# A grouped convolution in front of a routed linear layer: the first tiles convolved in plain float32, and the first three steps in another order

## What is computed

```python
out = lax.conv_general_dilated(x, weight, window_strides=(1,), padding=[(4, 4)],
                               dimension_numbers=('NCH', 'OIH', 'NCH'), feature_group_count=4)
y = out + einsum('nd,od->no', c, c_weight)[:, :, None] + bias[None, :, None]
base_out = einsum('btd,od->bto', y, base_W) + base_b            # 512 -> 512
probs = softmax(einsum('btd,nd->btn', y, router_W) + router_b)  # 15 routes
topk_p, topk_i = top_k(probs, 8)
w = einsum('btk,btke->bte', topk_p, onehot(expert_map[topk_i]))
h = einsum('btd,erd->bter', y, A)                               # 8 experts, rank 16
result = x + base_out + einsum('bter,eor->bto', h * w[..., None], B) * 2.0
```

## Time and profile before

| | us |
|---|---|
| median of 3 runs | 187.44 |
| lowest and highest | 187.42, 187.69 |
| the profiled execution | 188.49 |
| its span, first to last instruction | 186.7 |
| TensorE busy in it | 180.1 |
| DVE, POOL, ACT busy | 156.2, 143.9, 82.9 |

### The profile page before, as it was taken

One profiled execution on the slowest core, in us unless ns is written; L12 is line 12 of the kernel. 1 busy time (PEld: TensorE's weight loads), 2 busy tenths in 40 slices (PEclk: granted clock), 3 DMA queues, 4 the chain that ended last, 5 costly groups with the idle time before them and its releaser, 6 DMA issues.

```text
span 186.7 us, 3948 instructions
## 1 busy us (share of the span) xinstructions
PE 180.1 (96%) x1243; PEld 171.8 (92%) x1243; DVE 156.2 (84%) x513; ACT 82.9 (44%) x249; POOL 143.9 (77%) x141
## 2 busy tenths in 40 slices
PE   7889999999999999999999999999999999999992
PEld 2469979999999999999999999999999999999992
DVE  0997999989888888888888888889888889978673
ACT  3687344454343545444344545434354544422310
POOL 2639979988898888888988888879888887895410
PEclk9999999999999999999999999999999999999998
DMA  6999642755745454645555464754645631233313
GB/s 185 387 312 328 191 158 80 227 169 180 219 137 165 137 186 167 228 169 190 151 153 176 135 217 169 225 170 123 207 125 177 243 98 68 97 112 112 116 56 112
DMA packets 17733, 32.01 MB, mean 171 GB/s; under 512 B 1969, under 2 KB 2865, under 8 KB 17713
## 3 DMA queue, kind: packets, MB, share of 16 engines
...
## 4 chain that ended last, share of the span: by engine, by line
PE 88%; DVE 4%; DMA 2%; issue 2%; ACT 2%; DVEq 0%; SPq 0%
PE wide_ps L619 58%; PE wide_ps L655 11%; PE conv_banks L605 10%; PE edge_bank L605 2%; DMA wide_sb<-wide_w 2%; PE odd_bank L642 2%; PE conv_banks L619 2%; PE conv_banks L566 2%; ACT wide_hi L350 1%; DVE xr L768 1%; DVE y_lo L887 1%; DVE y L859 0%; PE conv_banks L655 0%; DVE y_rows L774 0%; ACT y_hi L394 0%
## 5 line engine op out<-in xcount | busy, mean ns | idle before, releaser
L619 PE MATMUL wide_ps<-wide_hi,y_hi 128*128 128x400 f32 (+1 forms) x248 | 79.2, 325 | 1.3 <-ACT y_hi L394 0.7
L619 PE MATMUL wide_ps<-wide_hi,y_lo 128*128 128x400 f32 (+1 forms) x248 | 75.9, 312 | 0.0
L619 PE MATMUL wide_ps<-wide_lo,y_hi 128*128 128x400 f32 (+1 forms) x248 | 75.9, 312 | 0.0
L496 POOL TENSOR_TENSOR terms_lo<-terms,terms_hi 128x512 fp32r<-128x512 f32 x28 | 36.3, 1298 | 18.6 <-ACT terms_hi L379 18.5
L619 PEld LDWEIGHTS wide_ps<-wide_hi,y_hi 128*128 128x128 f32 x248 | 46.3, 188 | 3.9 <-ACT y_hi L394 1.1
L619 PEld LDWEIGHTS wide_ps<-wide_lo,y_hi 128*128 128x128 f32 x248 | 46.5, 189 | 0.0
L619 PEld LDWEIGHTS wide_ps<-wide_hi,y_lo 128*128 128x128 f32 x248 | 46.4, 188 | 0.0
L491 POOL TENSOR_TENSOR xr<-xr,base_b_sb 128x512 f32<-128x512 f32 x32 | 41.9, 1310 | 3.8 <-DMA xr<-x_rows 3.8
L514 POOL TENSOR_TENSOR y_lo<-y,y_hi 128x512 fp32r<-128x512 f32 x29 | 37.5, 1295 | 3.2 <-ACT y_hi L394 3.2
L401 ACT ACTIVATE hw_hi<-odd_bank 128x128 fp32r<-128x128 f32 x31 | 8.6, 277 | 52.7 <-PE odd_bank L642 52.7
L768 DVE TENSOR_TENSOR xr<-wide_ps,xr 128x512 f32<-128x512 f32 x30 | 20.7, 691 | 5.4 <-PE wide_ps L655 4.1
...
## 6 DMA issues: line engine op xcount, KB each, us to landing
...
conv_sb<-conv_w ACTq DMA_DIRECT2D x2, 128.0 KB, 4.5
```

The costliest lines, as they stand in the source:

```text
L496: nc.gpsimd.tensor_tensor(terms_lo[i % 2][:, :, :, :], terms[i][:, :, :, :], terms_hi[i % 2][:, :, :, :].bitcast(F32), ALU.subtract)\
L619: mm = nc.tensor.matmul(sums_of(t, k)[:, b, 0:columns[1] - columns[0]], a[k % 2][:, r, :], w[:, r, columns[0]:columns[1]], start=r == 0 an ...
```

## The change

Tiles 0 to 3 are convolved from `x_in` and `conv_sb` as they were loaded, in plain float32: two matmuls a tile instead of six. `x_hi`, `x_lo` and the split of the weight blocks that only these tiles use are gone (`conv_hi` and `conv_lo` have 10 blocks instead of 14, with their own numbering `S_*`). The condition inputs and the weight blocks are one tensor in memory, so ACT issues one DMA of 450 columns where there were two of 256 and 194, and then piece 1. The condition weights are spread by ACT, group 0 apart; group 0's condition matmul stands between the two of tile 0, and `condition_first(0)` waits for that group alone. The first `y_hi` is a copy on DVE. `wide_lo` of run 0 is made on POOL. `up_lo`, one DVE instruction before, is a subtraction on POOL from `up_scaled`, a second scaled copy that ACT makes. `y_lo` of tile 2 is made on POOL. SP issues weight piece 3 before `x_in` 3, and `terms` 4 after a wait for the last `wide` run. The warm-up has eight matmuls. The other pieces are a new order of the first three steps; `isinstance(t, int)` was always true.

```diff
-WARM_UP = 9
+WARM_UP = 8
...
-W_OWN, W_REACH = (0, 2, 4, 6), (1, 3, 5, 7)
+W_OWN, W_REACH = (1, 2, 5, 6), (0, 3, 4, 7)
...
+COND = N + C + GROUPS + 2 * ROUTES
+W_PIECES = (slice(0, COND + 2 * P), slice(COND + 2 * P, COND + 4 * P),
+            slice(COND + 4 * P, COND + 8 * P), slice(COND + 8 * P, COND + 11 * P),
+            slice(COND + 11 * P, COND + 14 * P))
...
+S_OWN, S_SUM, S_QUARTERS, S_ALL = (0, 1, 5, 6), (2, 3, 7, 8), (4, 9), 10
+S_PIECES = ((slice(0, 2), slice(1, 3), (0, 1)), (slice(2, 5), slice(8, 11), (3,)),
+            (slice(5, 7), slice(5, 7), (2,)), (slice(7, 10), slice(11, 14), (4,)))
...
             load_x(2)
             sync.wait_ge(wide_in[1], 16)
+            load_conv(3)
             load_x(3)
+            sync.wait_ge(wide_in[3], 16)
             load_terms(START, 0)
-            sync.wait_ge(wide_in[3], 16)
-            load_conv(3)
             load_edges(START // 2, 0)
...
+            def cond_weights(groups):
+                nc.scalar.copy(cond_w_sb[:, groups, :, :],
+                               cond_w_in_sb[:, groups, :].unsqueeze(2)
+                               .to_broadcast([P, groups.stop - groups.start, BP, CG]))\
+                    .then_inc(cond_w_ready, 1)
...
+            act.wait_ge(conv_w_in[0], 16)
+            cond_weights(slice(0, 1))
+            cond_weights(slice(1, GROUPS))
+            wide_high(range(1))
+            bias_condition(range(1), 1)
...
             odd_up(START, 0)
-            y_high(1, 1)
-            conv_high(3)
-            bias_condition(1)
+            y_high(1, 1, 2)
+            bias_condition(range(2, GROUPS), 3)
             exponentials(0, 0)
             terms_high(START, 0)
             act.wait_ge(up_in, 16)
             nc.scalar.activation(up_hi[:, :], up_sb[:, :], ACT.Copy, scale=LORA_SCALE)\
                 .then_inc(up_hi_ready, 1)
+            nc.scalar.activation(up_scaled[:, :], up_sb[:, :], ACT.Copy, scale=LORA_SCALE)\
+                .then_inc(up_scaled_ready, 1)
             edge_high(START // 2, 0)
...
-                    conv_high(4)
+                if t == 1:
+                    conv_high(2)
...
+            pool.wait_ge(wide_hi_ready, 1)
+            wide_low_part(nc.gpsimd, 0, wide_lo_first)
...
+            def up_low():
+                pool.wait_ge(up_scaled_ready, 1)
+                pool.wait_ge(up_hi_ready, 1)
+                nc.gpsimd.tensor_tensor(up_lo[:, :], up_scaled[:, :], up_hi[:, :].bitcast(F32),
+                                        ALU.subtract).then_inc(up_lo_ready, 1)
+
+            conv_low(0)
+            conv_low(1)
             edge(START // 2, 0)
-            conv_low_later(3)
 
             def step(t, k, p, q):
-                if isinstance(t, int) and t == 0:
+                if t == 0:
                     terms_low(t + 4, k)
+                    up_low()
                     edge_low(p + 2, k // 2)
                     pool.wait_ge(base_b_in, 16)
                     bias_rows(t, k)
+
+                    y_low(t + 2, k + 2, 3)
                     return
-                if isinstance(t, int) and t == 1:
+                if t == 1:
+                    terms_low(t + 4, k)
                     bias_rows(t, k)
-                    terms_low(t + 4, k)
                     edge(p + 3, 1 - k // 2)
-
-                    y_low(t + 2, k + 2, 4)
-                    conv_low_later(4)
+                    y_low(t + 2, k + 2)
+                    conv_low(2)
+                    conv_low(3)
...
+            def conv_first(t):
+
+
+
+                own, reach = t % 2, 1 - t % 2
+                nc.tensor.matmul(first_ps[:, t % 2, :, :], conv_sb[:, W_OWN[t], :],
+                                 x_in[t][:, :, own:own + BLK], start=True, stop=False)
+                if t == 0:
+                    cond_sums(range(1), 1)
+                nc.tensor.matmul(first_ps[:, t % 2, :, :], conv_sb[:, W_REACH[t], :],
+                                 x_in[t][:, :, reach:reach + BLK], start=False, stop=True)\
+                    .then_inc(conv_done, 1)
...
-                    pe.wait_ge(odd_ready, 1)
+                    pe.wait_ge(odd_ready, 2)
...
+            for t in range(2):
+                pe.wait_ge(conv_w_in[t], 16)
+                pe.wait_ge(x_loaded[t], 16)
+                conv_first(t)
+            cond_sums(range(1, 2), 2)
+
+            def conv_later(t):
+                pe.wait_ge(y_rows_ready, t - 1)
+                pe.wait_ge(conv_w_in[2], 16)
+                pe.wait_ge(x_loaded[t], 16)
+                conv_first(t)
 
             def first_step():
                 runs = range(RUNS)
-                pe.wait_ge(y_hi_ready, 1)
+                pe.wait_ge(y_hi_first, 1)
                 for r in runs:
                     pe.wait_ge(wide_hi_ready, r + 1)
                     linear(0, 0, (r,), products=(HIGH,))
...
+                cond_sums(range(2, GROUPS), 2)
+                conv_later(2)
...
+                    pe.wait_ge(out_added, t - 1)
+                    if t == 2:
+                        pe.wait_ge(y_hi_ready, t + 1)
+                        linear(t, k, runs, (FRONT_BANK,), (HIGH,))
+                        linear(t, k, runs, (FRONT_BANK,), (W_REST,))
+                        pe.wait_ge(y_lo_ready, t + 1)
+                        linear(t, k, runs, (FRONT_BANK,), (Y_REST,)).then_inc(front_done, 1)
...
+            dve.wait_ge(conv_w_in[0], 16)
...
+            dve.wait_ge(cond_biased, 1)
             condition_first(0)
             turn(0, 0)
+            dve.wait_ge(y_ready, 1)
+            nc.vector.tensor_copy(y_hi[0][:, :, :], y[0][:, :, :]).then_inc(y_hi_first, 1)
+            y_low(0, 0)
             wide_low(1)
-            y_low(0, 0)
             wide_low(2)
             wide_low(3)
+            dve.wait_ge(cond_biased, 2)
             condition_first(1)
             turn(1, 1)
-            y_low(1, 1)
             choose(0, 0)
             dve.wait_ge(logits_ready, 1)
             best(0, 0)
...
-                    dve.wait_ge(up_hi_ready, 1)
-                    nc.vector.scalar_tensor_tensor(out=up_lo[:, :], in0=up_sb[:, :],
-                                                   scalar=LORA_SCALE,
-                                                   in1=up_hi[:, :].bitcast(F32), op0=ALU.mult,
-                                                   op1=ALU.subtract).then_inc(up_lo_ready, 1)
-                    hw_low(0, 0)
-                    y_low(2, 2)
                     dve.wait_ge(top_ready, 2)
                     mark(1, 1)
+                    condition_first(3)
+                    hw_low(0, 0)
+                    return
+                if t == 1:
                     difference(START + 1, 1)
-                    return
-                if isinstance(t, int) and t == 1:
+                    turn(3, 3)
                     add_out(0, 0)
                     weigh(1, 1)
-                    condition_first(3)
-                    turn(3, 3)
```

253 lines of the change are left out of this document (86 added, 167 removed).

## The result

| | before | after |
|---|---|---|
| median, runs on one chip | 187.7 | 186.8 |
| lowest and highest | 187.22, 188.39 | 185.62, 188.09 |
| ratio after / before | | 0.994 [0.9925, 0.9955] |
| profiled execution | 188.49 | 186.31 |
| its span | 186.7 | 184.5 |

The change makes the kernel faster, by 0.45 to 0.75%. The profiled execution, though, was forecast at 186.4 and took 186.31. So the document has two questions: which steps held inside the trace, and why the timed runs gained less than the pair of traces.

A forecast was written before the change was run, and what follows sets the result against it. TensorE's own work (96% busy) was taken to bound the steady part, so the start's gain would last: step 4, set by POOL, at 33.7 instead of 35.81, 2.1 us off the median 187.44, gives 185.3, range 184.6 to 186.8.

The forecast's parts named there:

- First weights and first linear: Start of the kernel: merged 450-column weight piece lands at 4.8 us, first `linear` matmul starts at 9.1 instead of 10.56.
- The cast on DVE: First `y_hi`, 0.43 us on DVE against 0.63 on ACT, plus 0.2 us held up by POOL's instruction.
- Plain convolutions: Tiles 0 to 3 on TensorE: 0.88 us per 512-column float32 matmul, 1.76 per tile against 1.43, +0.33 us each.
- Step 0 and 1: Reordered start on TensorE: `linear(0)` done at 12.75, tile 3 at 18.9; `turn_hw(0)`'s wait for `odd_up(5)` covered by 0.2 us.
- Step 2: On TensorE: begins at 22.2 instead of 24.05, without the wait for `add_out`, and lasts 5.13 us.
- Step 3: On TensorE: lasts 5.48 us, the length of a later odd step, against 5.74 before.
- Step 4: POOL's `y_lo(4)` sets its start at 33.7, after TensorE's 33.0, against 35.81 before; chance 0.42.
- The sum: Whole kernel: 35.81 - 33.7 = 2.1 us less, taken off the median 187.44, gives 185.3; profiled execution 186.4.
- The collision at `conv_lo(1)`: POOL's 384 columns start between DVE's `wide_lo(2)` and `wide_lo(3)`, delaying the latter 1.0 us: 186.3 us; chance 0.20.
- the rival of the clock: TensorE stays at the lower pace through tiles 0 and 1, +3.5 us there: 188.8 us; chance 0.06.
- The late landing: Merged weight piece lands at 5.5 or after, 0.7 us on the chain, POOL's stretch 18.6: 186.8 us; chance 0.09.
- POOL is not late: POOL's stretch under 17 us or started a microsecond sooner, so TensorE's own path decides: 184.6 us; chance 0.17.

The follow-up runs named there:

- the other four traces: The changed kernel profiled again, unaltered; these profiled executions took 187.03, 187.0, 186.64 and 187.76 us.
- POOL relieved: Changed kernel with POOL's `y_lo(4)` put ahead of `bias_rows(3)` in the fourth step (t == 3) alone: 186.75 us, ratio 0.9934 to the kernel before.
- TensorE relieved by 0.46 at step 3: Changed kernel with the old place of `odd_up(5)` back, `turn_hw(0)` waiting for `odd_up(4)` only: 186.57 us, ratio 0.9924 to the kernel before.
- the repeated trace: The kernel before, run again unaltered for a second trace: 188.05 us; profiled execution 187.82, span 186.0.

## Why the prediction was right inside one trace and wrong in the number

**First weights and first linear.** Forecast 4.8 and 9.1, measured 4.55 and 8.92. The merged piece landed 3.8 us after its issue, like the small one of the earlier trace rows (3.6). The cast on DVE was not held up (0.43 us; POOL's instruction ended at 8.50). That `y` was ready at 8.44, forecast 8.4, was luck: the weights came 0.25 early, and tile 0's first matmul took 0.2 too long. In the other four traces the first `linear` began at 9.18 to 10.06.

**Plain convolutions.** A record is 0.43 us (512-column rows 0.86 a matmul), forecast 0.44; the 128-column row was the right base.

**Step 0 and 1.** `linear(0)` ended at 12.77 (forecast 12.75). `turn_hw(0)`, covered by 0.2 in the forecast, waited 0.22, and in other executions nothing or 0.16 to 0.79: `odd_up(5)` stands behind `y_high(2)` on ACT, forecast at 18.7 and done at 19.18, as `odd_up(4)` before them had waited for its load. The cover was a matter of landing, and was too thin to be counted.

**Step 2.** Forecast 22.2, measured 22.59: the wait above, and step 1's own length. It took 5.14, as said.

**Step 3** was costed at 5.48 and took 5.81. This is a mis-sized term: it was taken from a later odd step, and here `up` waits for `hw_lo`, which stands behind the turn on DVE. Before had the same stall, in its 5.74.

**Step 4** was to be set by POOL at 33.7. POOL's stretch began at 15.95 (forecast 15.9) and took 17.28 (17.8), so y_lo(4) ended at 33.23, and TensorE's own chain ended at 33.54. The number came out by luck, as TensorE was 0.5 later than forecast and POOL 0.5 sooner; the mechanism was a tie that TensorE led. With POOL relieved nothing moved. With TensorE relieved by 0.46 at step 3, 0.27 was left at step 4, which began 0.15 behind POOL's y_lo(4).

**The sum.** The profiled execution was forecast at 186.4 and took 186.31; the four other traces of the changed kernel read 186.64 to 187.76, so that hit too is in part luck. The step that failed is "35.81 - 33.7 = 2.1 us less" with "the gain is taken off the median: 185.3". Both starts of step 4 were taken as one moment. The traces showed 35.81 and 35.22 in the kernel before, and 33.54 to 34.87, 34.1 on average, in the changed one: a gain of 1.4 us. The 2.1 was the gain against a late execution of before (188.49, typical 188.01), with a wait for `add_out` that the repeated trace does not have; on the side of after it held nothing for the slow first matmul and the collision. And it was subtracted from the median of three early executions (187.44). From 185.34 to the typical 186.66 it is 1.32 us: 0.57 for the median of three (188.01 - 187.44), 0.48 for the late trace of before, 0.35 for the trace of after, which was an early one (186.66 - 186.31), less 0.08 by which the pair of traces gained more than 2.1. The 1.05 us between the profiled execution and the median, which the table of before shows, was half the forecast gain; it should have been asked which of the two was typical.

**The rivals.** The collision at `conv_lo(1)` was real, with the mechanism and nearly the price given (forecast 1.0 us; it was 0.7 on DVE and 0.5 on TensorE in four traces, 1.2 and 1.1 in the fifth), but as something that happens in some executions. So was the rival of the clock, at least its slow pace: not for tiles 0 and 1 as a whole, +3.5, but for tile 0's first matmul and the small one behind it, 0.1 to 1.2 us. Both were given a chance as cases of which one comes true; they come and go from execution to execution, and so are in every median. The late landing did not come. "POOL is not late" came in half: its stretch took 17.28 and TensorE's own path decided, but that path was 0.5 us longer than its 33.0.
